# Post-norm network of two blocks, block 1: order of the score rows, width of the loads of the mix back, one semaphore, and the beats

## The reference

```python
dots = jnp.einsum('hg,bgij->bhij', W_pre_th, dots)
dots = jnp.where(causal[None, None], mask_value, dots)
vk = jax.lax.top_k(dots, TOPK)[0][..., -1:]
dots = jnp.where(dots < vk, mask_value, dots)
attn = jax.nn.softmax(dots, axis=-1)
attn = jnp.einsum('hg,bgij->bhij', W_post_th, attn)
```

## Time and profile before

| what | value |
|---|---|
| three executions | 3629.79, 3636.32, 3643.66 us |
| the profiled execution | 3643.09 us, span 3641.8 us |
| granted clock of TensorE, mean | 0.981 of full |
| busy: PE, DVE, ACT, POOL | 3402.0, 3429.3, 3094.4, 1742.1 us |

### The profile page before, as it was taken

One profiled execution on the slowest core, in us unless ns is written; L12 is line 12 of the kernel. 1 busy time (PEld: TensorE's weight loads), 2 busy tenths in 40 slices (PEclk: granted clock), 3 DMA queues, 4 the chain that ended last, 5 costly groups with the idle time before them and its releaser, 6 DMA issues.

```text
span 3641.8 us, 78829 instructions
## 1 busy us (share of the span) xinstructions
PE 3402.0 (93%) x19351; PEld 2539.4 (70%) x19351; DVE 3429.3 (94%) x18632; ACT 3094.4 (85%) x10837; POOL 1742.1 (48%) x3670
## 2 busy tenths in 40 slices
PE   4999999996999999999999999999999999999987
PEld 2888888873666666666666666666666666676665
DVE  7999999945999999999999999999999999999993
ACT  5888888856899898999999898998889989889863
POOL 0000000004666666666666666666666666666663
PEclk9999999997899999999999999999999999999998
DMA  3000000003222222222222222222222222222210
GB/s 132 11 14 13 13 13 13 10 8 85 68 74 71 76 83 66 65 65 65 67 65 65 73 70 71 74 69 76 77 73 66 65 65 65 67 65 65 73 55 4
DMA packets 254142, 210.76 MB, mean 58 GB/s; under 512 B 78000, under 2 KB 234736, under 8 KB 252912
## 3 DMA queue, kind: packets, MB, share of 16 engines
q1 hardware_dynamic: 253680, 205.70, 18.2%
HBM read 93.97 MB, written 111.67 MB: 56 GB/s over the span
## 4 chain that ended last, share of the span: by engine, by line
PE 64%; DVE 15%; ACT 14%; issue 3%; POOL 2%; DMA 0%; SPq 0%; DVEq 0%; ACTq 0%; POOLq 0%
PE bank L363 12%; PE bank L221 8%; PE bank L1415 5%; DVE W L1807 5%; PE bank L1403 5%; PE bank L1388 4%; DVE last L1829 3%; PE bank L331 3%; PE bank L1446 3%; PE bank L195 3%; PE bank L453 3%; PE bank L1480 3%; ACT SN L1599 3%; PE bank L1460 2%; PE bank L1419 2%
## 5 line engine op out<-in xcount | busy, mean ns | idle before, releaser
L1807 DVE MATCH_REPLACE8 W<-last,W 128x130 f32<-128x130 f32 (+18 forms) x3456 | 871.0, 259 | 0.0
L1829 DVE MAX8 last<-W 128x8 f32<-128x130 f32 (+18 forms) x3456 | 762.0, 261 | 0.1
L1914 POOL TENSOR_SCALAR posts<-post,share 128x128 f32<-128x128 f32 x1024 | 366.0, 379 | 284.2 <-DVE share L1736 279.7
L1583 ACT ACTIVATE T<-T,peak 128x260 f32<-128x260 f32 (+15 forms) x1024 | 410.9, 409 | 4.2 <-POOL T L1965 3.0
L1599 ACT ACTIVATE SN<-bank,rq 128x260 f32<-128x260 f32 (+1 forms) x1024 | 357.9, 424 | 61.4 <-PE bank L1388 59.7
L1403 PE MATMUL bank<-T,pre 128*128 128x40 f32 (+15 forms) x1024 | 366.1, 440 | 14.1 <-ACT T L1607 9.8
L1415 PE MATMUL bank<-posts,T 128*128 128x128 f32 (+7 forms) x2048 | 311.9, 289 | 69.1 <-POOL posts L1914 60.8
L1965 POOL TENSOR_TENSOR T<-T,below 128x520 f32<-128x520 f32 (+12 forms) x416 | 360.8, 884 | 19.9 <-DVE below L1838 4.6
L1415 PEld LDWEIGHTS bank<-posts,T 128*128 128x128 f32 (+7 forms) x2048 | 249.4, 174 | 165.5 <-POOL posts L1914 89.7
L921 DVE TENSOR_TENSOR_SCAN hs<-dA,dx 128x256 f32<-128x256 f32 x512 | 348.5, 681 | 4.7 <-ACT dA L783 1.9
L1930 POOL TENSOR_TENSOR T<-T,w_mask 128x32 f32<-128x32 f32 x512 | 141.2, 279 | 415.9 <-ACT T L1607 413.5
(11 more groups left out here) (243 smaller groups left out, 9571.9 us busy)
## 6 DMA issues: line engine op xcount, KB each, us to landing
scores_by_token<-SN SPq DMA_DIRECT2D x64, 520.0 KB, 3.0
scores_by_token<-SN SPq DMA_DIRECT2D x64, 396.0 KB, 3.6
scores_by_token<-SN SPq DMA_DIRECT2D x32, 780.0 KB, 3.3
scores_by_token<-SN SPq DMA_DIRECT2D x32, 264.0 KB, 2.7
scores_by_token<-SN SPq DMA_DIRECT2D x32, 260.0 KB, 2.3
T<-scores_by_token SPq DMA_DIRECT2D x32, 244.0 KB, 2.9
T<-scores_by_token SPq DMA_DIRECT2D x32, 228.0 KB, 3.1
T<-scores_by_token SPq DMA_DIRECT2D x32, 212.0 KB, 4.0
```

The source lines that it names most:

```text
L1583: act.activation(one, one, ACT.Exp, bias=peak[k % 2][:, j:j + 1], accum_out=total[k % 4][:, j:j + 1]).then_inc(e_made, 1)
L1807: dve.match_replace(both[:, s, at:to], best[n], both[:, s, at:to], LOWEST).then_inc(ranked, 1)
L1829: dve.max(best[n], both[:, s, at:to]).then_inc(ranked, 1)
L1914: pool.tensor_scalar(posts[(4 * k + j) % NP][:], post[:], share[k % 2][:, j:j + 1], 1.0, ALU.mult, ALU.mult).then_inc(posts_made, 1)
```

## The change

- `QUAD` stands ahead, and `LAID` gives a new order of the groups in `T8`: the four groups of a quad are adjacent (`0, 1, 31, 30`; then in quads 1 and 2 the narrow pair first, in quads 3 to 6 the wide pair first; `16, 17, 15, 14` last). `T8` keeps its size. Pair 14/15 is swapped too, so it is fetched by two transfers.
- `mix_back`: `tall` loads 128 columns wherever the quad's columns in `T8` go that far, also past the end of the group's own row, and fewer only at the end of the quad. The result's further rows are not copied by `at_keep`, which is unchanged. In quads 0 to 2 the order of the six matmuls changes to that of the others.
- The second pair instruction (line 1787) counts on a semaphore of its own, `paired`, and no more on `ranked`. The fold at line 1812 waits for it, and so does each masking product of GpSimd, for the pair instructions of the next quad.
- Most beats of TensorE, many of ScalarE and GpSimd have other numbers; those of VectorE do not.

```diff
--- before.py
+++ after.py
@@ -1104,9 +1104,15 @@
     def width(g):
         return seen_by(g | 1)
 
-    ROW = [sum(width(k) for k in range(g)) for g in range(GROUPS + 1)]
-    ROW[GROUPS - 2:GROUPS] = ROW[GROUPS - 2] + KEYS, ROW[GROUPS - 2]
-    T8 = room.sbs("T8_", [P, ROW[GROUPS]], 2)
+    QUAD = [(30 - 2 * i, 31 - 2 * i, 2 * i, 2 * i + 1) for i in range(QUADS)]
+    LAID = [(0, 1, 31, 30)] + [(*q[2:], *q[:2]) if q[2] < HALF // 2 - 2 else q for q in QUAD[1:-1]] + [(16, 17, 15, 14)]
+    LAID = [g for four in LAID for g in four]
+    ROW = [sum(width(k) for k in LAID[:LAID.index(g)]) for g in range(GROUPS)]
+    T8 = room.sbs("T8_", [P, sum(width(g) for g in range(GROUPS))], 2)
+
+    def quad_end(i):
+
+        return max(ROW[g] + width(g) for g in QUAD[i])
 
     def pair_scores(b, g):
         at = min(ROW[g], ROW[g + 1])
@@ -1124,7 +1130,6 @@
     def side(g):
         return int(ROW[g] > ROW[g ^ 1])
 
-    QUAD = [(30 - 2 * i, 31 - 2 * i, 2 * i, 2 * i + 1) for i in range(QUADS)]
     PREMIX = [list(range(HALF)), [g for i in range(QUADS) for g in (30 - 2 * i, 31 - 2 * i)]]
     PAIR_AT = {g: (blk * HALF + k) // 2 for blk in range(2) for k, g in enumerate(PREMIX[blk])}
 
@@ -1163,7 +1168,7 @@
     s_made, s_kept = sems.sem("s_made"), front.s_kept
     premixed, t_kept, masked = sems.sem("premixed"), sems.sem("t_kept"), sems.sem("masked")
     ranked, peaked, turned, e_made, shared = (sems.sem(n) for n in ("ranked", "peaked", "turned", "e_made", "shared"))
-    topped = sems.sem("topped")
+    topped, paired = sems.sem("topped"), sems.sem("paired")
     found_wide, found_narrow = sems.sem("found_wide"), sems.sem("found_narrow")
     marked, dropped = sems.sem("marked"), sems.sem("dropped")
     cut_marked = sems.sem("cut_marked")
@@ -1200,6 +1205,10 @@
         b, i = divmod(k, QUADS)
         return CUT_ALL * b + sum(len(c) for c in CUT[:i]) + sum(x <= j for x in CUT[i])
 
+    def pairs_by(b, i):
+
+        return (QUADS + 1) * b + i + (1 if i < QUADS - 1 else 2)
+
     def mark_of(g, j0):
         return below[j0 // 2][:, 0:2 * width(g)].rearrange("p (two n) -> p two n", two=2)
 
@@ -1210,68 +1219,68 @@
         return DROPS_ALL * b + sum(len(c) for c in DROPS[:i]) + sum(x <= j for x in DROPS[i])
 
 
-    PE_K = (-16, -9, 13, 14)
-    PE_K_TURN = (13, 31, 33, 36)
-    PE_Q = (24, 33, 39, 41)
-    PE_Q_SUM = (40, 40, 46, 46)
-    PE_Q_TURN = 53
-    PE_ATTEND = (16, 16, 21, 22)
-    PE_GATES = (43, 49, 55, 55)
-    PE_MIX = (56, 68, 84, 111, 118, 120, 124, 138)
-    PE_OUT = 35
+    PE_K = (-18, -12, 12, 13)
+    PE_K_TURN = (12, 27, 30, 37)
+    PE_Q = (28, 29, 38, 40)
+    PE_Q_SUM = (40, 40, 44, 45)
+    PE_Q_TURN = 47
+    PE_ATTEND = (16, 19, 22, 25)
+    PE_GATES = (43, 46, 51, 52)
+    PE_MIX = (57, 78, 86, 108, 114, 118, 127, 137)
+    PE_OUT = 31
     PE_VAR1 = 39
-    PE_SPREAD1 = 47
-    PE_W1 = 53
-    PE_W2 = 55
-    PE_H1 = (56, 58, 61, 62)
-    PE_H2 = (63, 71, 86, 90)
-    PE_SCORE0 = (55, 56, 59)
-    PE_W3 = 99
-    PE_SCORE1 = (67, 78, 84, 98, 100, 103, 107, 107)
-    PE_VAR2 = 105
-    PE_SPREAD2 = 114
-    PE_V = (121, 123, 124, 128)
-    PE_PREMIX = [[71, 80, 85, 90, 101, 110, 111, 116], [122, 123, 132, 142, 147, 169, 188, 189]]
-    ACT_K = (-8, -1, 32, 38)
+    PE_SPREAD1 = 45
+    PE_W1 = 48
+    PE_W2 = 53
+    PE_H1 = (60, 64, 69, 72)
+    PE_H2 = (75, 81, 88, 92)
+    PE_SCORE0 = (56, 63, 68)
+    PE_W3 = 96
+    PE_SCORE1 = (78, 84, 87, 95, 100, 102, 104, 106)
+    PE_VAR2 = 102
+    PE_SPREAD2 = 112
+    PE_V = (120, 121, 130, 132)
+    PE_PREMIX = [[83, 85, 91, 94, 100, 107, 110, 113], [123, 126, 133, 143, 149, 170, 195, 202]]
+    ACT_K = (-8, -1, 33, 38)
     ACT_K_TURN = (42, 44, 49, 52)
-    ACT_Q = (46, 49, 57, 59)
+    ACT_Q = (46, 49, 58, 59)
     ACT_K_ROOT = (3, 39)
     ACT_Q_SUM = 59
     ACT_Q_ROOT = 64
-    ACT_PEAK = (11, 52, 55, 65, 76, 94, 95, 116)
-    ACT_WIDE = (45, 64, 66, 83, 85, 95, 118, 142)
-    ACT_NARROW = (49, 64, 67, 84, 89, 109, 123, 150)
+    ACT_PEAK = (10, 46, 54, 65, 73, 94, 96, 117)
+    ACT_WIDE = (45, 64, 66, 83, 88, 95, 118, 142)
+    ACT_NARROW = (49, 64, 67, 85, 89, 109, 123, 143)
     ACT_MIX = (79, 87, 90, 115, 119, 130, 139, 157)
     ACT_SQUARE1 = 49
-    ACT_ROOT1 = 56
+    ACT_ROOT1 = 57
     ACT_GATES = (59, 61, 62, 63)
-    ACT_SILU = (59, 61)
+    ACT_SILU = (61, 61)
     ACT_SCORE0 = (64, 74, 77)
-    ACT_H1 = (77, 79)
+    ACT_H1 = (77, 78)
     ACT_H2 = (92, 94)
     ACT_SCORE1 = (86, 88, 89, 95, 96, 98, 108, 110)
     ACT_SQUARE2 = 95
     ACT_ROOT2 = 103
-    ACT_V = (138, 141, 151, 151)
-    ACT_PREMIX = [[87, 88, 93, 94, 97, 110, 115, 126], [129, 131, 157, 166, 184, 195, 202, 207]]
+    ACT_V = (135, 137, 151, 151)
+    ACT_PREMIX = [[87, 88, 92, 94, 97, 110, 110, 126], [129, 131, 157, 166, 184, 191, 202, 207]]
     DVE_SHARE = (57, 80, 91, 99, 104, 118, 125, 136)
-    POOL_GATES = (49, 56, 57, 64)
-    POOL_OPEN = (91, 105, 126, 139)
-    ACT_CTX = (40, 42, 43, 44)
+    POOL_GATES = (29, 31, 36, 36)
+    POOL_OPEN = (90, 105, 123, 139)
+    ACT_CTX = (41, 42, 43, 44)
     DVE_END1 = 56
     DVE_Q_CLIP = 64
     DVE_GATED = (66, 69)
     DVE_END2 = 119
-    POOL_TURN = (-40, -40, -40, -1, 12, 80, 87, 88)
-    POOL_SHARE = (71, 83, 90, 98, 104, 126, 129, 135)
-    POOL_DROP = (20, 65, 73, 78, 84, 94, 116, 132)
-    POOL_ROOT1 = 69
-    POOL_Q_ROOT = 76
-    POOL_ROOT2 = 118
-    POOL_PREMIX = [[92, 94, 95, 97, 112, 117, 120, 128], [130, 140, 145, 174, 196, 210, 212, 214]]
+    POOL_TURN = (-40, -40, -40, -4, 15, 72, 84, 89)
+    POOL_SHARE = (56, 79, 90, 100, 105, 122, 131, 142)
+    POOL_DROP = (22, 38, 57, 66, 81, 94, 111, 134)
+    POOL_ROOT1 = 50
+    POOL_Q_ROOT = 65
+    POOL_ROOT2 = 116
+    POOL_PREMIX = [[92, 100, 102, 107, 118, 119, 123, 128], [131, 143, 151, 159, 177, 201, 203, 220]]
     ACT_K_SCALE = (25, 42)
-    POOL_K_CLIP = (2, 23)
-    POOL_K_ROOT = (6, 44)
+    POOL_K_CLIP = (4, 26)
+    POOL_K_ROOT = (10, 27)
 
     def ctx_of(c2):
 
@@ -1410,25 +1419,25 @@
             if n:
                 pe.wait_ge(at_kept, AT_KEEPS * b + KEPT[i])
 
+            def tall(j, c):
+                m = min(quad_end(i) - ROW[QUAD[i][j]] - c, P)
+                return scores(b, QUAD[i][j], c, c + m), m
+
             def first(j):
-                m = min(width(QUAD[i][j]), P)
-                return pe.matmul(at0[0:m, j * P:(j + 1) * P], scores(b, QUAD[i][j], 0, m), posts[(n + j) % NP][:], start=True, stop=True)
+                x, m = tall(j, 0)
+                return pe.matmul(at0[0:m, j * P:(j + 1) * P], x, posts[(n + j) % NP][:], start=True, stop=True)
 
             def second(j):
-                m = min(width(QUAD[i][j]), 2 * P) - P
-                return pe.matmul(at1[0:m, j * P:(j + 1) * P], scores(b, QUAD[i][j], P, P + m), posts[(n + j) % NP][:], start=True, stop=True)
-
-            order = [(first, 0), (first, 1)]
-            if width(QUAD[i][2]) <= P // 2:
-                order += [(second, 0), (second, 1), (first, 2), (first, 3)]
-            else:
-                order += [(first, 2), (first, 3), (second, 0), (second, 1)]
-            for one, j in order:
+                x, m = tall(j, P)
+                return pe.matmul(at1[0:m, j * P:(j + 1) * P], x, posts[(n + j) % NP][:], start=True, stop=True)
+
+            for one, j in ((first, 0), (first, 1), (first, 2), (first, 3), (second, 0), (second, 1)):
                 last = one(j)
             for j in (1, 3):
                 if QUAD[i][j] in (HALF - 1, GROUPS - 1):
                     c = P if QUAD[i][j] == HALF - 1 else 2 * P
-                    last = pe.matmul(at1[0:MEM, 2 * P:3 * P], scores(b, QUAD[i][j], c, c + MEM), posts[(n + j) % NP][:], start=True, stop=True)
+                    x, m = tall(j, c)
+                    last = pe.matmul(at1[0:m, 2 * P:3 * P], x, posts[(n + j) % NP][:], start=True, stop=True)
             last.then_inc(back_mixed, 4)
 
         def attend(b, c2):
@@ -1782,16 +1791,15 @@
             if j0 == 2:
                 dve.wait_ge(found_narrow, len(TURNED) * (b + 1))
             dve.tensor_tensor(both[:, :, 0:h], x[:, :, 0:h], x[:, :, h:w], ALU.max).then_inc(ranked, 1)
-            paired = count = count + 1
+            larger = count = count + 1
             yield
-            dve.tensor_tensor(both[:, :, w:w + h], x[:, :, 0:h], x[:, :, h:w], ALU.min).then_inc(ranked, 1)
-            count += 1
+            dve.tensor_tensor(both[:, :, w:w + h], x[:, :, 0:h], x[:, :, h:w], ALU.min).then_inc(paired, 1)
             yield
             found, removed = [0, 0], [0, 0]
             rows = [(j, side(QUAD[i][j])) for j in (j0, j0 + 1)]
             best = [top[k % 2][:, j, :] for j, _ in rows]
             for n, (j, s) in enumerate(rows):
-                dve.wait_ge(ranked, paired)
+                dve.wait_ge(ranked, larger)
                 dve.max(best[n], both[:, s, 0:h]).then_inc(topped if j == last else ranked, 1)
                 found[n] = count = count + (j != last)
                 yield
@@ -1809,6 +1817,7 @@
```

(3 more changed lines are left out.)

## The result

The changed kernel takes 3654.01 us in the median of ten runs (3646.51 to 3665.30), the one before 3637.75 (3629.79 to 3643.66): a ratio of 1.0052, 95% interval [1.0042, 1.0062]. It is slower by 16 us, where 10 us less were forecast, and it lies above the range. The profiled execution took 3648.7 us.

The account below looks back on a forecast made before the run. Block 1 was taken as bound by VectorE's rankings, its idle time the possible gain. Terms 4 + 4.8 + 1 = 10 us off 3643.1 gave 3633, or 3626 on the median's scale; range 3608 to 3651.

Parts of the forecast that it names:

- the first rival: All of VectorE's waits go, the reordering winning beyond the loads: 19.8 us, 3616 us; chance 0.20.
- The wide loads: Mix back: stalls at narrow loads disappear, net 1.25 us of TensorE per sequence, about 39 us over all.
- the rival by which the load's width counts: Mix back: wider loads exposed, 2.4 us more a sequence, 72 us, 3708 us; chance 0.03.
- I assume that the drops stay: TensorE's clock drops for a few us in six periods; assumed unchanged when counting the late norms' 4.8 us.
- The 4.8 us for six late norms: Six periods with clock drops: VectorE waits 1.06 us for the last norm; a 0.8 us lead wins 4.8 us.
- the 4 us there: Boundary between sequences: first masked pair of half 1 copied 0.14 us earlier in 30 sequences, 4 us won.
- the 1 us for exponentials: VectorE's 2.6 us of waits for exponentials, after a clock drop or by chance: 1 us won.
- V piece 1 ahead of the premix: TensorE, before half 1's first premix: the piece delays it 1.0 us, cancelled by a 1.0 us lead from the loads.
- my far end: Boundary between sequences: if no lead arrives to pay for V piece 1, 25 us lost over 30 sequences.
- The wait on pairs: VectorE's fold and GpSimd's masking products: costs nothing; avoiding blocks of pair instructions buys 1 us at most.
- Gate 3's opening: GpSimd opens gate 3 ahead of share 7: at most 1.27 us of the gate's product, taken as nothing.
- The rival of a block in every sequence: A GpSimd instruction other than the masking product begins just before a pair instruction: 31 us, 3667 us; chance 0.05.

Follow-up runs that it names:

- With the clock held: Changed kernel with idle TensorE passes (fillers) in its two waits, 12 before quad 7's mix back and 6 before the last score piece: 3620.3 us, 0.9953.
- one filler: Changed kernel, V piece 1 and gate 3's opening in old places, twelve idle passes before quad 7's posts wait alone: 3632.1 us, 0.9985.
- the same passes elsewhere: Changed kernel with the same 18 idle passes in front of quad 2's mix back, where TensorE does not wait: 3692.4 us, 1.0152.
- the run with both beats put back: Changed kernel with V piece 1 behind the first premix of half 1 and gate 3's opening behind share 7 again: 3644.1 us, 1.0016.

## Why the prediction was wrong

*What bounds the kernel.* Right. With the clock held VectorE waits 0.8 us in 30 sequences, works 84.17 us of a period of 84.46, and the time is 3620 us: the floor that the first rival put at 3616.

*The wide loads.* Right in size: 39 us of TensorE's work were forecast and 38.9 are gone; that the two agree so closely is in part luck, since the drops, 17 against 6, lengthen TensorE's busy time too. With the clock held it is 1.2 us a sequence for the 1.25 forecast. Passes follow each other at 0.11 us with 128 columns loaded. The time of all weight loads grew by 48.7 us (PEld in the page) and stayed hidden: the rival by which the load's width counts falls. That the saving reaches the end was right as well, but only with the clock held: there it is 20 us, more than I had for it, as it also moves VectorE's fold out of the opening's way.

*"I assume that the drops stay".* This is the step that failed. I had read the rows of a drop for what it costs and not for what stands ahead of it, in the same view of the kernel before:

```profile
1438.08 1.01 PE L1388 MATMUL bank<-kT,qT 64*128 64x260 f32 x4 [0.65 <-ACT SN L1599]
```

The drops went from 6 to 17, and in the changed kernel each costs 1.7 us. Shown is that they hang on the waits: fillers in both take all of them away, one filler takes away those at its place, and the same passes elsewhere leave 15. Not shown is why the wait for `SN`, no longer than before, is now followed by a drop in every second sequence. With less work and VectorE's pace TensorE's busy share of the steady stretch falls from 95.9% to 94.2%, but that share does not sort the runs: it is 94.0% with the 8 drops of the wide loads alone, and 95.3% with the 29 of the run with both beats put back. A rival is the rhythm of the periods. In the kernel before the last five drops are each 256.00 us apart, in the changed one 13 of the 16 distances are 170.67 us, with both beats put back 27 of 28 are 85.33 us: three, two and one times the same number. The periods fit: three of the kernel before from one drop to the next make 255.8 to 256.1 us, two of the changed one 170.6 to 170.8 us, one with both beats put back mostly 85.31 to 85.34 us. So a few tenths of a microsecond in a period may decide how often the same wait is followed by a drop, whatever took them away. No run varies that alone.

The 4.8 us for six late norms came (no `x_d` wait is left), and another price took their place: behind a drop, a wait of 0.84 us at the boundary, so the 4 us there did not come (10.6 us before, 11.8 us after). Nor did the 1 us for exponentials (2.6 and 3.2 us).

*V piece 1 ahead of the premix.* Right, with wrong evidence at first sight. The boundary wait is over 0.4 us, which I had named as a sign against me; but putting the piece back does not help (1.0046), and with the clock held the wait is gone with the piece ahead. The lead pays for it, but not as I had worked it out. In the old order the same lead leaves the boundary wait as it was (0.35 us with the clock held), and with the new order it takes all of it away, over 10 us where I had 4. Why is open. Without the lead (narrow loads, clock held) the wait is 0.22 us and not the 1.2 us that my far end and the expectation for narrow loads with the new order had: the new order wins more elsewhere than I had seen.

*The wait on pairs.* "Nothing" was right for its cost (0.9999). "1 us at most" for what it buys was wrong by far: I looked for blocks in the kernel before, found none, and did not ask where the products would stand once TensorE, and with it the score copies, ran earlier. It buys 18 us with the wide loads and 55 to 93 us with the new order as well.

*Gate 3's opening.* "I take nothing" was wrong: 0.35 us of block in every second sequence, and 0.27% by the run that puts it back. I had asked who waits for the opening's queue, and not which VectorE instruction it would meet. The rival of a block in every sequence had the right kind, at a third of the price: the opening lasts 0.61 us and the product that made 1.02 us lasts 1.27. The Trainium skill (SBUF — State Buffer, Who interferes with whom) has a VectorE instruction with two SBUF inputs and a GpSimd one that reads SBUF exclude each other for a whole instruction; the rows agree: the fold begins 0.14 us behind the opening and ends 0.28 us after it.

*The sum.* Against the forecast of 3626 the clock costs most: holding it takes the changed kernel from 1.0052 to 0.9953, 36 us, and the kernel before only from 1 to 0.9989, 4 us. With the clock held in both, the change wins 13 us, near the 10 that were forecast; part of that is luck, since the boundary wait gave more than its term and there are no late norms left to win. Of VectorE's own account between the two profiles, 4 us fewer waits stand against 10.7 us more of blocks (6.1 by the opening, 3.6 by a gate's product in two periods around 2700 us, where one drop was twice as long and each took 87.3 us). That is most of the 9 us by which the 30 periods are longer; filling and tail are 4 us shorter. The profiled execution is among the fastest of its kernel, so that most have lost more to the clock than it shows: of the ten times the shortest, 3646.5 us, has a mean granted clock of 0.978, the longest, 3665.3 us, one of 0.970.

## What to carry to other kernels

Work taken from an engine that is not the bottleneck ends up as waiting, and on TensorE a wait, here one of 0.65 us in an engine that was 94 to 96% busy, can be followed by a fall of the clock: look at what stands ahead of each drop before you count a saving there, and if need be fill the wait with idle passes. Where VectorE is the bottleneck, each GpSimd instruction that is moved has to be placed against VectorE's two-input instructions, not only against its own queue; a semaphore that holds it back by half a microsecond can be free and worth percents. When two changes help only together (loads, order, wait, clock), test each of them with the others in place.

## What the hardware showed that was not expected

- The clock fell behind waits of TensorE as short as 0.65 us. The wait does not decide it alone: at 1779.27 us stands the same wait of 0.65 us as at 1693.47, in the next period, and the clock stays at 1.00. The Trainium skill (TensorE: Matmul & The Clock Gate, The HAM clock gate) says that the throttled clock is the default and that activity releases it. The fillers agree: 17 drops without them, none with them; the same passes elsewhere left 15, so their place counts. What exactly decides in one period and not in the next was not settled.

```profile
1779.27 0.71 PE L1397 MATMUL bank<-kT,qT 64*128 64x260 f32 x4 [0.65 <-ACT SN L1608]
```

- 18 idle passes of 2 us in all, per sequence, made the whole kernel 1% faster in the waits and 1% slower elsewhere.
- The number of drops says little about the time: 28 of them stand in a run of 1.0025 (opening put back) and 17 in one of 1.0052. A drop cost 1.7 us where VectorE's boundary wait and the block by the opening followed it, and 0.8 to 0.9 us with both beats put back.
- The fastest version of this study is the changed kernel with the fillers, with or without the two beats put back: 3620 us, 0.995 of the kernel before.
